# Joined table lookups, a tenth table on chip, and layers that follow their own chunk

## The reference

```python
e = jnp.stack([tbl_0[ids[:, 0]], tbl_1[ids[:, 1]], ..., tbl_25[ids[:, 25]]], axis=1)
combined = jnp.concatenate([dense_features[:, None, :], e], axis=1)
interactions = jnp.einsum('bnd,bmd->bnm', combined, combined)
z = jnp.concatenate([dense_features, interactions[:, _TRIU_I, _TRIU_J]], axis=1)
h = jnp.concatenate([z, dense_features], axis=1)
h = jnp.maximum(h @ W_top1 + b_top1, 0.0)     # 607 x 512
h = jnp.maximum(h @ W_top2 + b_top2, 0.0)     # 512 x 256
y = h @ W_top3                                # 256 x 1
```

## Time and profile before

| | |
|---|---|
| median of 3 runs | 377.36 us (376.21 to 377.71) |
| span of the profiled execution | 375.2 us, from the first to the last instruction; the median of the runs is 2.2 us more |
| PE busy | 329.8 us, 88% |
| weight loads (PEld) | 297.8 us, 79% |
| DVE, ACT, POOL busy | 198.1, 191.4, 258.0 us |
| granted clock of PE | 0.968 in the mean |

### The profile page before, as it was taken

How to read it: one execution, slowest core, us unless ns; L and a number is a source line. 1 busy time by engine, 2 the same in 40 slices (tenths; PEclk the granted TensorE clock), 3 DMA queues, 4 the chain that set the end, 5 groups by cost and what they waited for, 6 DMA issues and landing times.

```text
span 375.2 us, 13452 instructions
## 1 busy us (share of the span) xinstructions
PE 329.8 (88%) x6048; PEld 297.8 (79%) x6048; DVE 198.1 (53%) x364; ACT 191.4 (51%) x234; POOL 258.0 (69%) x280
## 2 busy tenths in 40 slices
PE   0476856999989999999999999999899988999797
PEld 0475745998779978997799878997799867997586
DVE  3599741995049901993079704990099405940000
ACT  2587633456544655455444653465535563455323
POOL 6777777777777777777777777777777777774000
PEclk9998985999999999999999999999999999999969
DMA  6997492663236623662266324752266225423140
GB/s 158 258 260 183 119 317 55 140 207 90 51 91 148 199 52 76 141 211 63 61 141 198 92 59 96 191 145 59 70 149 196 73 54 127 112 56 71 35 67 2
DMA packets 55415, 45.72 MB, mean 122 GB/s; under 512 B 39444, under 2 KB 45179, under 8 KB 55359
## 3 DMA queue, kind: packets, MB, share of 16 engines
q1 hardware_dynamic: 45783, 26.91, 28.8%
q0 software_dynamic: 8704, 17.84, 18.0%
q10 hardware_dynamic: 871, 0.11, 0.2%
HBM read 37.91 MB, written 6.93 MB: 120 GB/s over the span
## 4 chain that ended last, share of the span: by engine, by line
PE 52%; POOL 25%; issue 12%; ACT 4%; DVE 3%; DMA 3%; ACTq 1%; SPq 0%; DVEq 0%
PE banks L441 27%; POOL rows L399 25%; PE banks L460 7%; PE mlp L479 6%; PE moved L424 5%; PE mlp L489 4%; PE mlp L520 2%; DVE masks L682 2%; DMA hot_ids<-in_ids_of_field_dram 1%; DMA rows<-in_tbl_dram,ids_sb 1%; ACT vectors L771 1%; DVE low L669 1%; ACT vectors L754 1%; PE banks L531 1%; PE mlp L500 1%
## 5 line engine op out<-in xcount | busy, mean ns | idle before, releaser
L399 POOL DMA_INDIRECT rows<-in_tbl_dram,ids_sb x272 | 257.1, 945 | 83.8 <-issue 81.1
L682 DVE TENSOR_TENSOR masks<-hot_ids,row_of 125x512 fp32r<-125x512 int32 (+1 forms) x336 | 181.5, 614 | 17.9 <-PE banks L441 13.4
L441 PE MATMUL banks<-masks,high 125*128 125x256 f32 x592 | 151.3, 295 | 18.9 <-DVE low L669 18.9
L441 PE MATMUL banks<-masks,low 125*128 125x256 f32 x592 | 146.9, 287 | 0.0
L441 PEld LDWEIGHTS banks<-masks,high 125*128 125x128 f32 x592 | 116.2, 196 | 20.9 <-issue 16.3
L441 PEld LDWEIGHTS banks<-masks,low 125*128 125x128 f32 x592 | 116.3, 196 | 0.1
L771 ACT ACTIVATE vectors<-moved 128x384 f32<-128x384 f32 (+1 forms) x80 | 87.8, 1097 | 3.9 <-PE moved L424 3.5
L754 ACT ACTIVATE vectors<-banks 128x512 f32<-128x512 f32 (+1 forms) x40 | 44.6, 1114 | 77.8 <-PE banks L441 77.8
L460 PEld LDWEIGHTS banks<-vectors 128*27 128x27 f32 x4096 | 45.6, 107 | 29.7 <-issue 23.1
L460 PE MATMUL banks<-vectors 128*27 128x27 f32 x4096 | 54.8, 196 | 14.5 <-issue 10.2
L691 DVE COPY vectors<-dense_sb 128x256 f32<-128x256 f32 x8 | 3.5, 435 | 103.1 <-PE banks L460 103.1
(11 more groups left out here) (33 smaller groups left out, 56.6 us busy)
## 6 DMA issues: line engine op xcount, KB each, us to landing
hot_ids<-in_ids_of_field_dram SPq DMA_DIRECT2D x32, 256.0 KB, 5.1
scratch<-products SPq DMA_DIRECT2D x28, 169.0 KB
rows<-in_tbl_dram,ids_sb POOLq DMA_INDIRECT x272
features<-scratch SPq DMA_DIRECT2D x7, 351.0 KB
w_sb<-in_tbl_dram SPq DMA_DIRECT2D x3, 448.0 KB
scratch<-products SPq DMA_DIRECT2D x28, 42.2 KB
dense_sb<-in_dense_dram SPq DMA_DIRECT2D x8, 128.0 KB, 4.8
hot_ids<-in_ids_of_field_dram SPq DMA_DIRECT2D x8, 128.0 KB
```

What stands on the lines that cost most here:

```text
L399: pool.indirect_dma_start(rows[:, (tile * TILE_ROWS + v) % RING, :], None, tables[f][:, :], bass.IndirectOffsetOnAxis(ap=ids_sb[:, tile, f ...
L441: last = nc.tensor.matmul(banks[:, j % BANKS, m * CHUNK:(m + 1) * CHUNK], part[:, part_of(j * PAIR + m, k), :], masks[:, mask % MASK_RING, ...
L682: nc.vector.tensor_tensor(masks[:, mask % MASK_RING, 0:size], hot_ids[0:PART_ROWS, n % ID_RING, 0:size], row_of[0:PART_ROWS, row:row + 1]. ...
```

## The change

- **Tables.** Two tables of 1250 rows are on chip now instead of one, ten tables with the eight of 1000. Sixteen fields are gathered for a tile, except in the two tiles of chunk 0, which gather the two long ones too (18). The rows ring has 24 places, the batches have four rows.
- **Units.** A lookup (a unit) has one table and the samples of two neighbouring chunks, so a matmul has 512 columns and a mask still 125 x 512. The tables are in two sets of five; between the multiply steps of chunk p stand the units of one set, for chunks p + 1 and p + 2, with the other set having been worked for p and p + 1. The first set at the start and the last at the end have one chunk and 256 columns.
- **PSUM.** The four `banks` become `looked` (two banks, for lookups) and `crossed` (two, for products), each used in turn. `vectors` has room for four tiles.
- **Order.** In `chunk(p)` PE works the multiply steps of chunk p, with two lookups between them, then three lookups, then all layers of chunk p itself but the last. ACT, DVE and SP follow that order.
- **Masks.** The ring has seven places.

```diff
-LONGS = [f for f in range(FIELDS) if ROWS[f] == LONG][:1]
+LONGS = [f for f in range(FIELDS) if ROWS[f] == LONG][:2]
...
-BATCH_SIZES = (4, 4, 3, 3, 3)
-RING = TILES * TILE_ROWS
-TILE_SLOTS = 3
+FIRST_SIZES, LATER_SIZES = (4, 4, 4, 3, 3), (4, 4, 4, 4)
+RING = 24
+TILE_SLOTS = 2 * TILES
+FIRST_SET, SECOND_SET = (2, 3, 4, 5, 1), (6, 7, 8, 9, 0)
+TABLES = FIRST_SET[:-1] + SECOND_SET + FIRST_SET[-1:]
-MASK_RING = 8
+MASK_RING = 7
...
+def set_of(k):
+    return SECOND_SET if k % 2 else FIRST_SET
+def chunks_of(k, h):
+    return [c for c in (k - 1, k) if 0 <= c < CHUNKS and (c > 0 or h >= len(LONGS))]
+UNITS = [(h, chunks_of(k, h)) for k in range(CHUNKS + 1) for h in set_of(k) if chunks_of(k, h)]
...
 SP, after the tables:
             sp.wait_ge(low_made, HOT)
...
-            load_dense(1)
-            for j in range(HOT_PAIRS):
-                load_hot_ids(1, j)
+            for u in units_of(2):
+                load_hot_ids(u)
+            def chunk(p):
+                u = units_of(p + 3) if p + 3 <= CHUNKS else [len(UNITS)] * len(FIRST_SET)
+                load_hot_ids(u[0])
+                load_dense(p + 2)
+                load_hot_ids(u[1])
+                write_products(p)
+                store_y(p - 1)
+                load_pairs(p)
+                load_hot_ids(u[2])
+                load_hot_ids(u[3])
+                load_hot_ids(u[4])
...
+            def look_up(u):
+                h, _ = UNITS[u]
+                pe.wait_ge(low_made, TABLES.index(h) + 1)
+                if u >= 2:
+                    pe.wait_ge(unit_kept, u - 1)
+                for k in range(PARTS[h]):
+                    mask = FIRST_MASK[u] + k
+                    pe.wait_ge(mask_made, mask + 1)
+                    for part in (high, low):
+                        last = nc.tensor.matmul(looked[:, u % 2, 0:COLUMNS[u]], part[:, part_of(h, k), :],
+                                                masks[:, mask % MASK_RING, 0:COLUMNS[u]],
...
 PE, chunk 0:
             def first_chunk():
+                u = units_of(2)
                 multiply(0, 0)
+                turn(1, 3)
+                look_up(8)
                 multiply(0, 1)
                 turn(1, 4)
+                look_up(u[0])
                 multiply(0, 2)
                 multiply(0, 3)
...
 PE, the chunks after it:
+            def chunk(p):
+                b_now, a_next, b_next = TILES * p + 1, TILES * (p + 1), TILES * (p + 1) + 1
+                u = units_of(p + 2)
+                multiply(p, 0)
+                turn(b_now, 2)
+                look_up(u[0])
+                multiply(p, 1)
+                turn(b_now, 3)
+                look_up(u[1])
+                multiply(p, 2)
+                multiply(p, 3)
+                turn(a_next, 0)
+                last_layer(p - 1)
+                look_up(u[2])
+                turn(a_next, 1)
+                look_up(u[3])
+                turn(a_next, 2)
+                look_up(u[4])
+                turn(a_next, 3)
+                first_layer(p, 0)
+                first_layer(p, 1)
+                turn(b_next, 0)
+                first_layer(p, 2)
+                first_layer(p, 3)
+                second_layer(p, 0)
+                turn(b_next, 1)
+                second_layer(p, 1)
+            def last_chunk():
+                b_now = TILES * LAST + 1
                 multiply(LAST, 0)
+                turn(b_now, 2)
                 multiply(LAST, 1)
+                last_layer(LAST - 1)
+                turn(b_now, 3)
                 multiply(LAST, 2)
                 multiply(LAST, 3)
...
 ACT:
+            def keep_unit(u):
+                h, chunks = UNITS[u]
+                if chunks[-1] >= 2:
+                    act.wait_ge(step_ready, (chunks[-1] - 1) * CHUNK_STEPS)
+                elif chunks[-1] == 1:
+                    act.wait_ge(low_made, STAGED)
+                act.wait_ge(mask_used, FIRST_MASK[u + 1])
...
```

More of the change, by code:

```diff
@@ L206, in of_tile, with of_chunks @@
             return t % TILE_SLOTS * TILE
-        def of_chunk(c, v, count):
-            first, second = of_tile(TILES * c), of_tile(TILES * c + 1)
+        def of_chunks(chunks, v):
+            first = of_tile(TILES * chunks[0])
             whole = vectors[:, first:first + 1, v:v + 1]
-            return bass.AP(whole.tensor, whole.offset,
-                           [list(whole.ap[0]), [1, count], [(second - first) * VECTORS, TILES], [VECTORS, TILE]])
+            step = of_tile(TILES * chunks[-1]) - first
+            ap = [[VECTORS, CHUNK]] if len(chunks) == 1 else [[step * VECTORS, len(chunks)], [VECTORS, CHUNK]]
+            return bass.AP(whole.tensor, whole.offset, [list(whole.ap[0])] + ap)
         def write_quad(engine, c, q, written, half=None):
@@ L424, in turn @@
                     last = nc.tensor.transpose(moved[:, m * TILE:(m + 1) * TILE],
-                                               rows[:, (t * TILE_ROWS + v) % RING, :], identity[:, :])
+                                               rows[:, (rows_before(t) + v) % RING, :], identity[:, :])
                 last.then_inc(batch_ready, 1)
-            def look_up(c, j):
-                if c == 0:
-                    pe.wait_ge(low_made, PAIR * j + WIDTHS[j])
-                elif j < BANKS:
-                    pe.wait_ge(step_kept, (c - 1) * CHUNK_STEPS + j + 1)
-                if j >= BANKS:
-                    pe.wait_ge(pair_kept, c * HOT_PAIRS + j - BANKS + 1)
-                for k in range(PARTS[j]):
-                    mask = c * MASKS + FIRST_MASK[j] + k
-                    pe.wait_ge(mask_made, mask + 1)
-                    for m in range(WIDTHS[j]):
-                        for part in (high, low):
-                            last = nc.tensor.matmul(banks[:, j % BANKS, m * CHUNK:(m + 1) * CHUNK], part[:, part_of(j * PAIR + m, k), :],
-                                                    masks[:, mask % MASK_RING, m * CHUNK:(m + 1) * CHUNK],
-                                                    start=(part is high and m == 0 and k == 0),
-                                                    stop=(part is low and m == WIDTHS[j] - 1 and k == PARTS[j] - 1))
@@ L581, in second_chunk @@
+                second_layer(0, 0)
                 turn(3, 1)
[L582 to L609 removed]
+                second_layer(0, 1)
@@ L652, in _ @@
             pe.wait_ge(constants_made, CONSTANTS)
+            before_first()
             first_chunk()
-            second_chunk()
-            for i in range(2, LAST):
-                chunk(i)
+            for p in range(1, LAST):
+                chunk(p)
             last_chunk()
@@ L662, in _, with split @@
         def _(dve):
-            def split(h):
-                dve.wait_ge(high_made, h + 1)
-                dve.wait_ge(table_copied, h + 1)
-                for first, last, whole in ((0, COPIED_PARTS, copied), (COPIED_PARTS, PARTS[h // PAIR], stage(h))):
+            def split(n):
+                h = TABLES[n]
+                dve.wait_ge(high_made, n + 1)
+                dve.wait_ge(table_copied, n + 1)
+                for first, last, whole in ((0, COPIED_PARTS, copied), (COPIED_PARTS, PARTS[h], stage(h))):
                     if first < last:
@@ L965, in last_chunk @@
                 keep_step(LAST, 3)
+            before_first()
             first_chunk()
-            act.wait_ge(weights_loaded, 16 * WEIGHTS)
-            second_chunk()
-            for i in range(2, LAST):
-                chunk(i)
+            for p in range(1, LAST):
+                chunk(p)
             last_chunk()
```

578 lines of the change are left out of this document (267 added, 311 removed).

## The result

The changed kernel takes 420.95 us in the median of four runs (416.26 to 423.97), the kernel before 377.53 beside it. The ratio is 1.1055, interval 1.0988 to 1.1121; it leaves out the two runs counted as slow (423.97 and 423.66 us, granted clock 0.947 against 0.951 and 0.955). The other two have a mean of 417.25, and the profile is of the run of 423.97. I had forecast 395 and a range to 402. The sign was right, the size was not.

What follows compares the result with a forecast made beforehand. It took PE to bound early chunks (40.1 us) and POOL late ones (42.4). Start 106.8, five chunks 212.0, chunk 6 40.5 and end 33.9 gave a span of 393.2, plus 2.2: 395 us, range 379 to 402.

Steps and rivals of the forecast that it cites:

- PE's chunk: PE's work in one chunk: look-ups, multiply steps, layers, turns and a gap sum to 40.7 us if nothing waits.
- The look-ups: PE's 84 look-up matmuls of 512 columns in a chunk, at 0.219 us each from the layer steps: 18.4 us.
- the rivals' spacings: Look-ups on PE: weight loads set the spacing, so 512 columns pass in 0.12 us; 383 us in all, chance 0.03.
- the Trainium skill's 131 ns: Look-ups on PE: stated sustained spacing of 512-column matmuls with weight loads, which would make a chunk's look-ups 11.0 us.
- The new wait: Ahead of first_layer in each chunk: products take 15.4 us against 13.7 of cover, so PE waits 1.7 us (0 to 3.5).
- The rival of the hidden way: Chunks: the products' way takes 13.7 us or less, so the five waits of 1.7 go: 385 us, chance 0.12.
- The clock: Chunks: the granted clock falls at every wait, 5 × 1.6 us more, 403 us; chance 0.08.
- The start: Up to multiply(1,0): last split at 57.3 us, masks of later units from 67.7, multiply(1,0) at 106.8 (102 to 110).
- Chunk 6 and the end: Chunk 6, with units 256 wide and a wait of 6.5: 40.5 us; from multiply(7,0) to the store: 33.9 us.
- PE idle for 6 us ahead of the last layers: Last chunk: a sign that the forecast is right, PE standing idle 6 us before the last layers.
- The 0.55 between first and second layer: Each chunk: second layer directly follows first layer on PE, with a gap of 0.55 us between them.
- POOL was the bound: Whole kernel: POOL's shorter gather stream decides, 12 × 1.25 = 15 us off, 362 us; chance 0.10.

Runs made afterwards that it cites:

- steps apart: Changed kernel with its multiply steps kept apart, step 0 of the next chunk between first_layer and second_layer, the others between look-ups: 410.41 us, ratio 1.0839.
- a pair in before: Kernel before with multiply steps 2 and 3 of chunks 2 to 6 next to each other: 386.25 us, ratio 1.0252.
- four in a row: Changed kernel with all four multiply steps of a chunk side by side, ahead of the two look-ups that stood between them: 445.25 us, ratio 1.1754.
- the end of before apart: Kernel before with its last two multiply steps, multiply(7,2) and (7,3), separated by second layer and last layer work: 374.05 us, ratio 0.9885.
- Taking the ids ahead: Changed kernel with ids of units 9 to 13 loaded ahead of the weights, and the weight sum behind the masks: 412.75 us, ratio 1.0959.
- the last run: Kernel before, last two multiply steps apart, plus chunk 1's ids ahead of the weights and two look-ups between chunk 0's multiply steps: 378.5 us, ratio 1.0029.
- the two runs that should have isolated it: Changed kernel with multiply steps apart, products first and ids ahead; one long table's matmuls 32 columns wide: 407.25 us; its masks 32 wide too: 400.1 us.

## Why the forecast missed

By its own steps; the terms are 106.8 + 212.0 + 40.5 + 33.9, measured 117.6 + 230.4 + 41.4 + 32.6 (the windows above). The profiled span is 28.9 us over my sum: 10.8 at the start, 18.4 in the five chunks (2.5 each by stalls, 2.3 by look-ups, less 1.1 of the new wait), 0.9 in chunk 6, and 1.3 less at the end.

- **PE's chunk** is the step that failed. It took "four multiply steps of 1.80, 7.2" and asked what the change does to their sum, not to their neighbours. Idle time with no wait shown, which the sum has nowhere, is 2.5 us in the mean of five chunks, 2.3 of it inside the steps. The row was in the trace of before, in its last chunk (351.57 and 356.00 above), and I read past it. Shown by steps apart (-10.5 or -8.2), a pair in before (+9.2), four in a row (+24), the end of before apart (-4.3).
- **The look-ups**, 18.4 a chunk: measured 20.7 in the mean of five. The spacing is 0.2275 and not the layers' 0.219, which is 0.7; change-overs to other work are 0.8; the rest, 0.7, goes with the steps apart, where the clock stays at 1.00 in all five chunks, so I put it to the lower clock behind the stalls. With the steps apart 19.9 are left, 1.6 more than the 18.3 of before: the tenth table isn't free, as the joining gives back only some 3 us in the whole program. Of the rivals' spacings 0.12 did not occur; the Trainium skill's 131 ns (TensorE: Matmul & The Clock Gate, "Back-to-back issue gap") is far from the 227.5 ns here.
- **The new wait** was right in kind and too large: 0.6 us in the mean where I had 1.7. The way took 17.2 in chunk 1 (134.65 to 151.85) against my 15.4: writes 10.8 where I had 9.8, landing 4.4 where I had 3.3. But longer look-ups, slow behind the stall above all, lengthened its cover. 42.4 + 2.5 + 2.3 - 1.1 is the measured 46.1. The rival of the hidden way (0.12) was thus nearly right about the waits and brought no gain.
- **The clock** rival (0.08) was partly right: it falls in chunks 2, 3 and 5, though behind the stall, not behind the wait for features.
- **The start** was 10.8 us too early. The last split ended at 62.8 (mine 57.3, range to 59). Its masks began 11.4 behind it (mine 10.4). From there to multiply(1,0) 43.4 us (mine 39.1): in multiply(0,2) and (0,3) PE stalls for 2.81 too, while DVE, its seven places full, waits 3.77. Taking the ids ahead brought first_layer(0,0) 8.7 us forward in the mean of the profiles. Why the splits are 5.5 us later stays open.
- **Chunk 6 and the end** were right within 1.3 us, but not by their parts. In the last chunk I had PE idle for 6 us ahead of the last layers; it waited 3.2 for features, and stalls of 1.3 and 2.7 that I had not foreseen stood ahead of that. In chunk 6 the wait was 5.0 where I had 6.5, with a stall of 1.0. The 0.55 between first and second layer came true (0.56).
- **POOL was the bound** (0.10) fell. The kernel before waits for rows 0.79 and 1.71 us in its last two full chunks; the version with its end apart came to first_layer(0,0) 3.0 us later and to first_layer(6,0) only 0.2 later, with those waits nearly gone (0.2 in all). A lateness of 3 us at the start was thus taken up, while the further 5 of the last run were not. My estimate from that is that POOL and PE are within about 3 us of one another, and that twelve gathers less could give that much, not 15.

What stays open: what each edit is worth to the microsecond, since the changed kernel's own level is known to some 4 us only; and the price of the tenth table alone. The account gives 1.6 us a chunk by the look-ups' time; the two runs that should have isolated it changed the clock and DVE's part instead.

## What to carry to other kernels

Before moving blocks of many small matmuls next to one another, look in the trace for a place where two stand side by side already, and read the idle time inside the second. Put long instructions between them: what ran out here was instructions (256 in 1.8 us), while the engine was busy no more than elsewhere. Judge such an edit by the stall in the trace and by what waits in its place, and repeat the kernel it is compared with. A freed engine is worth only its distance to the next bound, here some 3 us by my estimate. And a leave-out run that makes an engine's work lighter can lower its clock: check the clock of the windows behind it before reading a price.

## What I had not expected of the hardware

- PE's own instructions come by DMA, about 256 in a transfer of 16.4 KB. When 256 are used up in 1.8 us the transfers still come 3.8 to 4.0 us apart (in four steps in a row; never under 3.2), and PE stands between them with no semaphore to wait for, until 2.2 to 3.2 us after one starts. At the start of before, in a slice of the page with 317 GB/s, such a stall was 4.15 us.
- PE's clock fell after 20 matmuls of 32 columns that stood 0.11 us apart without a gap, followed by a turn and a wait of 1.60 us in one chunk and 0.48 in another (granted 0.67 and 0.69 over the next 5.2 us). Waits of 1.4 us behind full look-ups left it at 1.00.
